# Carried sums of a graph kernel: one scan along (feature, step) in place of a chain of 16 instructions

## The reference, cut to what matters

```python
h = relu(layernorm(x))
# layer 0: attention over edges, 8 heads of 16 features, with a loop edge at every node
q, k, v = (layer_norm(h, g1, b1) @ W + b for W, b in (Wq, Wk, Wv))
e = sum(q[dst] * k[src], per head) / 4
p = exp(e - segment_max(e, dst))
agg = segment_sum(p * v[src], dst) / segment_sum(p, dst)
x = x + (h + agg @ Wo + bo + ffn(...))
# layer 1: a sum over neighbours and a two-layer perceptron
h = relu(layernorm(x))
neigh = segment_sum(h[src], dst)
x = x + relu(((1 + eps) * h + neigh) @ W1 + b1) @ W2 + b2
```

## Time and profile before

| what | us |
|---|---|
| median of 3 executions | 4883.41 (4882.2 to 4883.43) |
| the profiled execution, its own time | 4890.98 |
| its span, first to last instruction | 4889.3 |
| POOL (GpSimd) busy | 3449.5, 71% of the span |
| DVE (VectorE) busy | 2869.8, 59% |
| ACT (ScalarE) busy | 534.1, 11% |
| PE (TensorE) busy | 490.7, 10% |
| gathers of stage B after the first batch, start of first to end of last | 388.4 to 2366.3 |
| gathers of stage D | 2727.8 to 4718.2 |

### The profile page before, as it was taken

How to read it: one execution, slowest core, us unless ns; L and a number is a source line. 1 busy time by engine, 2 the same in 40 slices (tenths; PEclk the granted TensorE clock), 3 DMA queues, 4 the chain that set the end, 5 groups by cost and what they waited for, 6 DMA issues and landing times.

```text
span 4889.3 us, 25937 instructions
## 1 busy us (share of the span) xinstructions
PE 490.7 (10%) x2321; PEld 354.0 (7%) x2321; DVE 2869.8 (59%) x7335; ACT 534.1 (11%) x1354; POOL 3449.5 (71%) x3609
## 2 busy tenths in 40 slices
PE   4610000000000000000188200000000000000005
PEld 2410000000000000000166100000000000000003
DVE  7827988988888898888678222222222222222224
ACT  4400000000000000000166200000000000000001
POOL 4677777777777777777554577777777777777766
PEclk9655555555555555555599655555555555555558
DMA  9995666666666666666432233333333333333334
GB/s 362 381 362 174 215 212 213 216 214 212 212 211 214 212 217 211 212 211 214 130 86 81 76 103 103 103 103 104 103 103 103 103 103 103 104 103 103 103 97 137
DMA packets 233382, 810.42 MB, mean 166 GB/s; under 512 B 66752, under 2 KB 93408, under 8 KB 183102
## 3 DMA queue, kind: packets, MB, share of 16 engines
q1 hardware_dynamic: 79484, 463.98, 24.8%
q0 software_dynamic: 139072, 331.82, 23.7%
q10 hardware_dynamic: 14722, 13.70, 0.8%
HBM read 455.06 MB, written 354.21 MB: 166 GB/s over the span
## 4 chain that ended last, share of the span: by engine, by line
POOL 36%; issue 19%; DMA 17%; DVE 16%; DVEq 6%; PE 4%; ACT 1%; SPq 1%; POOLq 0%; ACTq 0%
POOL arena L628 36%; DVE arena L1822 10%; DMA q_edges<-arena 7%; DMA arena<-h_tab,idx 5%; DMA arena<-kv_tab,idx 3%; DVEq L1623 2%; PE ps L1227 2%; DMA states<-arena 2%; DVE arena L1578 1%; DVEq L1615 1%; DVE arena L1590 1%; PE ps L1238 1%; DVEq L1820 1%; DMA arena<-states,node_idx 1%; DVE ps L1655 1%
## 5 line engine op out<-in xcount | busy, mean ns | idle before, releaser
L628 POOL DMA_INDIRECT arena<-h_tab,idx x1568 | 1489.1, 950 | 530.5 <-issue 476.1
L628 POOL DMA_INDIRECT arena<-kv_tab,idx x1568 | 1486.8, 948 | 511.5 <-issue 506.6
L1822 DVE SCALAR_TENSOR_TENSOR arena<-arena,keep 128x128 f32<-128x128 f32 x1568 | 551.1, 351 | 1448.0 <-DMA arena<-h_tab,idx 1333.2
L1590 DVE SCALAR_TENSOR_TENSOR arena<-arena,keep,ps 128x128 f32<-128x128 f32 x1568 | 538.8, 344 | 87.1 <-issue 3.7
L1531 DVE SCALAR_TENSOR_TENSOR ps<-ps,keep,arena 128x128 f32<-128x128 f32 x1567 | 550.5, 351 | 18.8 <-issue 1.5
L628 POOL DMA_INDIRECT arena<-states,node_idx x196 | 193.9, 989 | 150.0 <-DVE node_idx L1766 89.7
L1578 DVE TENSOR_TENSOR arena<-arena,ps 128x1024 f32<-128x1024 f32 x196 | 230.5, 1218 | 56.6 <-DMA arena<-kv_tab,idx 56.1
L1123 ACT COPY idx<-src_all 128x16 int32 x96 | 19.6, 204 | 1942.9 <-DVE arena L1822 1942.9
L1655 DVE TENSOR_TENSOR ps<-arena,ps 128x2048 f32<-128x2048 f32 x98 | 224.4, 2289 | 0.0
L1618 DVE TENSOR_REDUCE ps<-arena 128x128 f32<-128x2048 f32 x98 | 224.1, 2287 | 0.1
L1197 PE MATMUL ps<-arena,ones 128*128 128x512 f32 x4 | 3.6, 1056 | 2062.5 <-DVE arena L1556 2062.5
(11 more groups left out here) (226 smaller groups left out, 1797.0 us busy)
## 6 DMA issues: line engine op xcount, KB each, us to landing
states<-arena SPq DMA_DIRECT2D x98, 1152.0 KB, 5.3
q_edges<-arena SPq DMA_DIRECT2D x98, 1024.0 KB, 6.1
arena<-q_edges SPq DMA_DIRECT2D x98, 1024.0 KB, 7.8
states<-arena SPq DMA_DIRECT2D x98, 1024.0 KB, 4.2
arena<-kv_tab,idx POOLq DMA_INDIRECT x1568, 2.8
arena<-h_tab,idx POOLq DMA_INDIRECT x1568, 2.6
kv_tab<-arena ACTq DMA_DIRECT2D x14, 896.0 KB, 11.5
arena<-kv_tab SPq DMA_DIRECT2D x14, 448.0 KB, 4.8
```

What stands on the lines that cost most here:

```text
L628: pool.indirect_dma_start(to, None, tab, bass.IndirectOffsetOnAxis(ap=at, axis=0)).then_inc(done, 16)
L1590: done = nc.vector.scalar_tensor_tensor(rows_n[:, b, :], rows_n[:, b - 1, :] if b else carried, keep[:, n * B + b:n * B + b + 1], weighed[ ...
L1822: done = nc.vector.scalar_tensor_tensor(rows[k][:, b, :], behind, keep[:, n * B + b:n * B + b + 1], rows[k][:, b, :], ALU.mult, ALU.add)
```

## The change

**Layout.** The buffers `q_now` and `weighed` in PSUM are turned from (step, feature) to (feature, step), so the 16 steps of one feature lie side by side. Weighed values are done in halves of 64 features. The score tiles move to PSUM banks of their own.

**Scans.** One `tensor_tensor_scan` over such a layout, with a gate tile `keep_flat` (the keeps of the batch repeated for 64 features, zero at step 0), computes the running sums of all its features: the zero stops the sum at each feature's border. The carried value of the batch before is added into step 0 by one small instruction (`begin_fill`, `begin_states`). The fill of the queries takes 6 scans of 256 or 512 elements, the states 2 of 1,024.

**ScalarE** makes the gate tile (`keep_features`), saves the last query (`q_last`), turns the loaded queries into PSUM (`turn_queries`, 2,048 elements), and turns the results back into `stb` (two copies of 1,024). The queries of batch n+1 can be turned only when the products of batch n have read the tile.

**Stage D** does the same with the gathered rows: ScalarE turns them into PSUM, VectorE adds the carry and runs two scans of 1,024 into `run_sums`, ScalarE turns them back into a separate store buffer `sums_b`. GpSimd waits for `rows_turned` in place of the store, and no longer for `carry_read` before the last row.

The diff, cut:

```diff
-        q_now = ps[:, 0:4, :].rearrange("p a (b f) -> p (a b) f", f=HID)
-        weighed = ps[:, 4:8, :].rearrange("p a (b f) -> p (a b) f", f=HID)
+        q_flat = ps[:, 0:4, :].rearrange("p a f -> p (a f)")
+        q_now = q_flat.rearrange("p (f b) -> p f b", b=B)
+        weighed_flat = ps[:, 4:6, :].rearrange("p a f -> p (a f)")
+        weighed = weighed_flat.rearrange("p (f b) -> p f b", b=B)
...
             def store_b(n, k):
-                sp.wait_ge(state_s, n + 1)
...
+                sp.wait_ge(stb_set, n + 1)
...
                     if not first:
-                        pool.wait_ge(weighed_s, n - 1)
+                        pool.wait_ge(weighed_s, (n - 1) * 2)
...
                     if not first:
-                        pool.wait_ge(sums_out[k], i * 16)
+                        pool.wait_ge(rows_turned, n - 1)
                     settle(pool)
                     for b in range(B):
-                        if b == B - 1 and not (first and k == 0):
-                            pool.wait_ge(carry_read, n)
-                            settle(pool)
                         gather(rows[k][:, b, :], h2_tab, idx[k][:, b:b + 1], rows_in[k])
...
+            def keep_features(n, k):
+                nc.scalar.copy(keep_by[k][:, :, 1:B], keep[:, bass.ds(n * B + 1, B - 1)].unsqueeze(1).to_broadcast([P, HF, B - 1]))
+
+            def turn_queries(k):
+                nc.scalar.copy(q_now, qb[k].rearrange("p b f -> p f b")).then_inc(q_turned, 1)
...
                     gates(n + 1, 1 - k)
-                    act.wait_ge(prod_s, n + 1)
-                    settle(act)
-                    nc.scalar.copy(idx[k][:], src_all[:, bass.ds((n + 2) * B, B)]).then_inc(idx_set, 1)
+                    keep_features(n + 1, 1 - k)
+                    if not last_batch(n):
+                        act.wait_ge(q_in[1 - k], i * 16 + 16 + (16 if k else 0))
+                        settle(act)
+                        act.wait_ge(prod_s, (n + 1) * 2)
+                        settle(act)
+                        nc.scalar.copy(q_last, q_now[:, :, B - 1])
+                        nc.scalar.copy(idx[k][:], src_all[:, bass.ds((n + 2) * B, B)]).then_inc(idx_set, 1)
+                        act.drain()
+                        turn_queries(1 - k)
...
+                    for half in range(2):
+                        act.wait_ge(state_s, n * 2 + half + 1)
+                        done = nc.scalar.copy(stb[k][:, :, half * HF:(half + 1) * HF].rearrange("p b f -> p f b"),
+                                              sums_flat[:, half * HF * B:(half + 1) * HF * B].rearrange("p (f b) -> p f b", b=B))
+                    done.then_inc(stb_set, 1)
...
+            def begin_fill(n):
+
+                dve.wait_ge(q_turned, n + 1)
+                nc.vector.scalar_tensor_tensor(q_now[:, :, 0], q_last, keep[:, n * B:n * B + 1], q_now[:, :, 0],
+                                               ALU.mult, ALU.add).then_inc(q_begun, 1)
+
+            def fill(n, f0, f1):
+
+                dve.wait_ge(q_begun, n + 1)
+                part = q_flat[:, f0 * B:f1 * B]
+                done = nc.vector.tensor_tensor_scan(part, keep_flat[n % 2][:, 0:(f1 - f0) * B], part, 0.0, ALU.mult, ALU.add)
...
+            def products(n, piece):
+
+                b0, b1 = piece * BH, piece * BH + BH
+                keys = kvb[n % 2][:, b0:b1, 0:HID]
+                nc.vector.tensor_tensor(keys, keys, q_now[:, :, b0:b1].rearrange("p f b -> p b f"), ALU.mult)\
+                    .then_inc(prod_s, 1)
...
+            def weigh(n, half):
+
+                values = kvb[n % 2][:, :, HID + half * HF:HID + half * HF + HF]
+                nc.vector.tensor_tensor(weighed.rearrange("p (h d) b -> p b h d", d=HD),
+                                        values.rearrange("p b (h d) -> p b h d", d=HD),
+                                        probs_h[:, half * NH // 2:(half + 1) * NH // 2, 1:CW].rearrange("p h t -> p t h")
+                                        .unsqueeze(3).to_broadcast([P, B, NH // 2, HD]), ALU.mult).then_inc(weighed_s, 1)
...
+            def states(n, half):
+
+                if n:
+                    dve.wait_ge(stb_set, n)
+                dve.wait_ge(carry_steps, n * 4 + half + 3)
+                nc.vector.tensor_tensor_scan(sums_flat[:, half * HF * B:(half + 1) * HF * B], keep_flat[n % 2],
+                                             weighed_flat, 0.0, ALU.mult, ALU.add).then_inc(state_s, 1)
...
+            def batch_d(n):
+
+                dve.wait_ge(sum_s, n * 2 + 1)
+                dve.wait_ge(rows_turned, n + 1)
+                nc.vector.scalar_tensor_tensor(rows_now[:, :, 0], run_sums.rearrange("p (f b) -> p f b", b=B)[:, :, B - 1],
+                                               keep[:, n * B:n * B + 1], rows_now[:, :, 0], ALU.mult, ALU.add)\
+                    .then_inc(carry_read, 1)
+                if n:
+                    dve.wait_ge(sums_set, n)
+                dve.wait_ge(carry_read, n + 1)
+                for half in range(2):
+                    part = slice(half * HF * B, (half + 1) * HF * B)
+                    nc.vector.tensor_tensor_scan(run_sums[:, part], keep1_flat[n % 2], rows_flat[:, part], 0.0,
+                                                 ALU.mult, ALU.add).then_inc(sum_s, 1)
```

More of the change, by code:

```diff
@@ L370, in build @@
         CW = B + 1
-        LATE = B - 4
-        BANK_STEPS = 4
+        BH = B // 2
+        HF = HID // 2
         cB = Carve(arena)
         qb = cB.two(B, HID)
-        diag8 = cB.take(NH, P)
-        masked = cB.take(NH, P)
-        weight = cB.take(NH, P)
-        weightT = cB.take(NH, P)
+        after_q = Carve(arena)
+        diag8 = after_q.take(NH, P)
+        masked = after_q.take(NH, P)
+        weight = after_q.take(NH, P)
+        weightT = after_q.take(NH, P)
+        assert after_q.at <= cB.at
+        keep_flat = cB.two(HF * B)
+        keep_by = [k.rearrange("p (f b) -> p f b", b=B) for k in keep_flat]
+        sums_flat = cB.take(HID * B)
         stb = cB.two(B, RW)
@@ L387, in build @@
         carried = cB.take(HID)
+        q_last = cB.take(HID)
         carry_max = cB.take(NH)
@@ L455, in build @@
         rows = cD.two(B, HID)
+        sums_b = cD.two(B, HID)
+        run_sums = cD.take(HID * B)
+        keep1_flat = cD.two(HF * B)
+        keep1_by = [k.rearrange("p (f b) -> p f b", b=B) for k in keep1_flat]
+        rows_flat = ps[:, 2:6, :].rearrange("p a f -> p (a f)")
+        rows_now = rows_flat.rearrange("p (f b) -> p f b", b=B)
+        rows_turned, sums_set = sem("rows_turned"), sem("sums_set")
         sameT = cD.take(P)
@@ L1582, in _ @@
-            for piece in range(PIECES):
-                products(0, 0, BW, piece)
-            nc.vector.tensor_copy(score[:, :, 0], top[:, :, B])
-            def state(n, b):
-                rows_n = stb[n % 2][:, :, 0:HID]
-                done = nc.vector.scalar_tensor_tensor(rows_n[:, b, :], rows_n[:, b - 1, :] if b else carried,
-                                                      keep[:, n * B + b:n * B + b + 1], weighed[:, b, :],
-                                                      ALU.mult, ALU.add)
-                if b == BANK_STEPS - 1:
-                    done.then_inc(scores_free, 1)
-                if b == B - 1:
-                    done.then_inc(state_s, 1)
@@ new lines, in begin_states @@
+            def begin_states(n, half):
+                dve.wait_ge(weighed_s, n * 2 + half + 1)
+                nc.vector.scalar_tensor_tensor(weighed[:, :, 0], carried[:, half * HF:half * HF + HF],
+                                               keep[:, n * B:n * B + 1], weighed[:, :, 0], ALU.mult, ALU.add)\
+                    .then_inc(carry_steps, 1)
+            def states(n, half):
[4 more added lines that the diff above has]
+                                             weighed_flat, 0.0, ALU.mult, ALU.add).then_inc(state_s, 1)
@@ L1671, in sums @@
-                fill_next(n, 6)
-                for b in range(2, LATE):
-                    dve.drain()
-                    state(n, b)
-                    if b + 5 < B:
-                        fill_next(n, b + 5)
-                    else:
-                        products_next(n, 0, 1)
-                    if last_batch(n) and b == B // 2:
-                        chunk_weights()
+                states(n, 0)
+                fill_next(n, 3)
+                if last_batch(n):
+                    chunk_weights()
@@ L1682, in _ @@
+                dve.wait_ge(state_s, n * 2 + 1)
+                weigh(n, 1)
+                fill_next(n, 4)
+                begin_states(n, 1)
+                fill_next(n, 5)
+                states(n, 1)
+            nc.vector.tensor_copy(score[:, :, 0], top[:, :, B])
             for n in range(BATCHES):
-                scores_and_probabilities(n)
+                probabilities(n)
                 sums(n)
-            for b in range(LATE, B):
-                dve.drain()
-                state(BATCHES - 1, b)
```

182 lines of the change are left out of this document (81 added, 101 removed).

## The result

| | us |
|---|---|
| changed kernel, median of 4 executions | 4929.5 (4928.99 to 4930.11) |
| kernel before, beside them, median of 4 | 4882.81 (4878.42 to 4883.43) |
| ratio, 95% interval | 1.0098 (1.008 to 1.0115) |
| changed kernel's profiled execution (span) | 4928.99 (4927.4) |

The change costs 46.7 us, 1%. The forecast was 82 us (4965), in a range from 4890 to 5260 with a chance of 0.86 for slower. The sign, the mechanism and the range held; the size was 35 us too high.

A forecast was written before the change was run, and what follows sets the result against it. It took POOL's gather pace, 20.39 us per batch in stage B, as the bound; a 21.0 us loop gave +72, stage ends +2 and +3.5, in all +77 to +78 on 4883.4, rounded to 4965; range 4890 to 5260.

The forecast's parts named there:

- What bounds the kernel: Stages B and D run at POOL's pace of issuing gathers; VectorE has 0.8 us per batch in hand in B.
- VectorE alone stays hidden: Stage B: VectorE's own work per batch goes from 20.2 to 20.3 us summed, 18.4 with overlap, still behind POOL.
- The loop of ScalarE and VectorE: Stage B: ScalarE's 7.3 us plus VectorE's 13.7 from begin_fill to states make 21.0 per batch, 0.6 over POOL's 20.39.
- The far read of ScalarE: Turning queries from SBUF at steps of 512 bytes takes 3.5 us, with 1.9 kept for the rivals.
- Edges: Costs outside the batches: +2 us before the first products, +2 at the end of B, +3.5 at the end of D.
- as long as before, plus turning back: End of stage B: the chain keeps its length and turning the results back adds 2 us.
- Stage D at 20.3 us per batch as before: Stage D keeps POOL's pace, since the turn, carry, scans and turning back fit beside 20 us of gathers.
- dropping the wait for `carry_read` gains nothing: Stage D: removing POOL's wait for that signal gains nothing, since POOL did not wait there.
- The rival "faster": Stages B and D: VectorE's two-SBUF-tensor instructions hold up gathers; at most 22 us gained, less 10 of edges: 4872; chance 0.03.
- The rival on PSUM: Stage B: VectorE pays for 64-byte steps in products and weigh; 5270 us, or 5080 to 5170 if one; chance 0.37.
- Edges only, 4893: Loop under 19.5 us, POOL bounds both stages, only edges cost: 4893 us, 0.2% slower; chance 0.18.
- The signs named ahead: Scans of 1.2 and 2.3 us, turn near 3.5, VectorE idle 2 to 3 before begin_fill, POOL in B waiting.

The follow-up runs named there:

- e1: Changed kernel with stage B's query turn reading SBUF packed and writing PSUM at steps of 64 bytes; 4880.83 us against 4880.48 for the kernel before.
- e7: Kernel before with the second tensor of stage D's chained instructions taken from PSUM, leaving out the neighbour sum; 4884.66 us against 4891.23 for the kernel before.
- before again: Second profile of the unchanged kernel before, one execution, for its trace on this chip; 4882.59 us, span 4881.0.
- e9: Changed kernel with ScalarE's two gate copies issued one batch earlier, behind the copy of the denominators; 4896.16 us against 4881.64 for the kernel before.
- e4: Kernel before with the change in stage D alone; 4876.84 us against 4880.48 for the kernel before.
- e8: Kernel before with stage D of the change, its turn reading SBUF packed and writing PSUM far; 4887.82 us against 4891.23 for the kernel before.

## Why the prediction was right, and where its size was off

**What bounds the kernel: right.** POOL's own pace bounded both stages, and VectorE had 0.8 us per batch in hand in stage B. e1 shows it from the other side: with the loop at some 19.0 us the rest of the change takes the time of before.

**VectorE alone stays hidden: right.** The scans cost 2.07 ns per element, not 1.04, as taken from the one short scan. Forecast and found: 512 elements 1.23 and 1.208 us; 1,024 elements 2.29 and 2.261 in stage B, 2.274 in D.

**The loop of ScalarE and VectorE: right as a mechanism, 0.3 us too long.** Forecast 7.3 + 13.7 = 21.0, found 7.22 + 13.48 = 20.70 in one batch and 20.71 on average. Of the 0.3, ScalarE's part has 0.08 and VectorE's 0.22. The term that failed is VectorE's 13.7: the six pieces of the fill measured 0.014 to 0.017 less apiece, 0.09 together, the state scans 0.03 apiece, the three short scans 0.04 together, the rest lies in small ones and in overlap; against it the carry took 0.355 instead of 0.279 (L1702). No term is off by as much as 0.1, but the loop was set against a pace only 0.7 us shorter, so 97 x 0.29 = 28 us came of it. A sum of 24 means with 1% each cannot give such a difference closely; the range of that case, 20.6 to 21.7, held it.

**The far read of ScalarE: right.** Taken 3.5 of 1.9 or 3.5, found 3.60; turning back taken 1.85 each, found 1.93. The choice by the nearest row held (a far write of ScalarE for a far read), and it decided the sign: at 1.9 the kernel is e1 and costs nothing.

**Edges.** The start was +2, found +1.9 (the first products at 403.56). The end of stage D was +3.5, found +3.9: turn 3.59, carry 0.44, scans 4.46, turning back 1.92. The end of stage B was +2, found +0.4. The step that failed called that chain "as long as before, plus turning back". Turning back costs 1.9 there as forecast, but VectorE's part is shorter: its last state scan ends 19.3 us behind the start of the last products (2412.55 to 2431.88), the last link before the change 21.9 (2368.17 to 2390.05).

**Stage D at 20.3 us per batch as before: wrong.** It runs 7 us faster in all, 20.20 (1980.0 / 98) against 20.27 (1986.9 / 98). The sentence "dropping the wait for `carry_read` gains nothing" holds by itself (e7 keeps that wait and is as fast). The step that failed is that stage D's pace was then taken as unchanged and the contention put at nothing in the sum; it measured 7 us. The rival "faster" named the cause, VectorE's instructions with two SBUF tensors, and capped it at 1568 x 8 ns = 12.5 us for D; it should have stood in the sum as a term of about half that, not only in a rival of 0.03. Its other part, up to 9 us in stage B, was nothing: the gathers of keys and values take 945 ns on average in before again and 946 in the changed kernel. The sign of it was there: the longest gather of stage D took 1072 ns, that of stage B 989.

**The rival on PSUM: wrong, at a chance of 0.37.** It would have cost 200 to 390 us; the products and the weighing cost 1207 and 1211 ns at steps of 64 bytes, not 2.3 us. Two rows on 8 elements each spoke against it and were right. The rule of the Trainium skill behind it ("Advanced Engine Details and Errata", Memory Cachelines) gives PSUM lines of two fp32 values and speaks of matmuls; carried over to VectorE and ScalarE it does not hold here. For SBUF, lines of 16 bytes, the trace agrees: ScalarE pays 3.60 instead of 1.87 us.

**"Edges only, 4893": not what happened**, but nearly what e9 (4896) and e1 (4881) take once the loop is short enough.

**The signs named ahead** came in: long scans at 1.21 and 2.26, the turn at 3.60, VectorE idle 2.63 ahead of `begin_fill` by ScalarE, POOL in B behind the weighing (69 waits).

**The 35 us by which the forecast was high** are, within 1 us: 22 from the 97 batches (forecast 97 x 21.0 = 2037.0 against 1967.4, so +69.6; found +47.5, which is 28 less for the shorter loop and 6 more because the profiled execution of before was 6 us slower there than before again), 7 from stage D, 1.6 from the end of B, and 4 to 5 from rounding up. The stretches that are left nearly cancel.

## What to carry to other kernels

When work is moved from a busy engine to an idle one, count the new loop from hand-over to hand-over, not the busy shares: here VectorE got 81 us less to do and the kernel got 46.7 us slower, because 7.2 us of ScalarE came to stand between two batches of VectorE. Where two layouts meet in a copy by ScalarE, try it with the packed side in SBUF and the far side in PSUM: here one line was worth the whole loss. And where an engine's pace is the floor, check what its neighbours read: two SBUF tensors in VectorE's instructions made the gathers of stage D 0.35% slower.

## What the runs showed of the hardware beyond what was expected

- A copy by ScalarE from SBUF to PSUM pays for far steps in SBUF and not for those in PSUM: 2,048 elements read at steps of 512 bytes and written packed take 3.60 us; read packed and written at steps of 64 bytes in PSUM, 1.87 us (e1). The two steps differ in length as well as in side; no run has ScalarE at steps of 64 bytes in SBUF or of 512 in PSUM, so what the length has in it is not shown. Read at steps of 64 bytes from PSUM, 128 elements take 263 ns (`q_last`, L1044), no more than the packed 295 of the earlier trace rows.
- VectorE pays nothing for steps of 64 bytes in PSUM, reading (1207 ns) or writing (1211). In SBUF it seems to pay for reading: the carry (L1702) takes 355 ns at steps of 64 bytes, 279 packed; and the first step of stage D, which reads its carry at such steps, takes 438 ns where `begin_fill`, the same form with a packed carry, takes 355. Both give 0.6 ns more per element. No run changed that alone, so it is read from rows and not tested (the page, part 5):

```profile
L1863 DVE SCALAR_TENSOR_TENSOR ps<-arena,keep,ps 128x128 f32<-128x128 f32 x98 | 42.9, 438 | 1498.9 <-ACT ps L1156 1498.9
...
L1572 DVE SCALAR_TENSOR_TENSOR ps<-arena,keep,ps 128x128 f32<-128x128 f32 x97 | 34.4, 355 | 252.2 <-ACT ps L1027 252.2
```

- The contention of VectorE's two-tensor instructions with POOL's gathers does not move the median gather (944 ns with and without). It makes those that run beside the chain longer, 955.5 ns on average against 943.6 in before again, one or two of a hundred of them much longer (up to 1034, 1058 and 1072 in the three profiles), and adds 7 us to 1,568.

Left open: what the gap of about 2 us after every 112 gathers is, which stage D has in every kernel here. A copy of e1 with stage B's chain end shortened, or with a third set of gate tiles to take `keep_features` off the loop too, was not tried; with POOL's pace as the floor neither should gain more than the edges. No version here that computes the whole result is faster than the kernel before by more than its interval; the nearest are e4 and e8, the change in stage D alone, at -3.6 and -3.4 us. For more, the pace of the gathers would have to change.
